# Convolution of a fused recurrent kernel: products over 64 rows on both halves of PE in place of products over 128 rows with a zero block

## The chip, the cores and the metric

One NeuronCore of one Trainium2 chip. The metric is the device time of one execution in microseconds, median of three runs. The kernel is bound by TensorE (PE), which holds a stationary operand of up to 128 x 128 and streams a moving operand through it. VectorE (DVE), ScalarE (ACT) and GpSimd (POOL) do the elementwise work, SyncE (SP) issues all DMAs.

## The reference, cut to what matters

Two layers over x of shape (128 batch, 128 time, 512 channels), float32. The change touches the first one, and in it the convolution, its projection, and the order of a few steps at the end of the projection.

```python
# layer 0: K = 128 taps, conv_w = cond (128 taps, 512 channels), N = 64
x_pad = jnp.pad(x, ((0, 0), (K - 1, 0), (0, 0)))
conv = conv_b + sum((x_pad[:, k:k + L, :] * conv_w[k, 0] for k in range(K)))
proj = conv @ Wp + bp
B_t = jax.nn.softplus(proj[..., :N])
C_t = jnp.tanh(proj[..., N:])
u = x @ Ws + bs
state = decay * state + dt * b_t * u_t        # scan over 128 steps, y = c_t * state
x = x + y @ Wo + bo
# layer 1
h_next = jnp.tanh(h @ Wh + x_t @ Wx + b)      # scan over 128 steps
x = x + h
```

The convolution is causal and depthwise, and has as many taps as there are time steps: for each channel it is a product of a lower triangular Toeplitz matrix (128 x 128) with x of that channel (128 times x 128 batch).

## The kernel before, in words

The program has two stages. The first (up to about 298 us) computes the convolution and its projection for all times into `bc` (128 rows x 16384, in SBUF), in four chunks of 128 channels. The second (from about 298 us to the end) walks the 32 groups of four time steps through both recurrences. The change touches the first stage only.

**Convolution** (`convolution`, lines 717 to 737). For each channel there is one float32 matmul: the stationary operand is `x_ring` (128 times in reverse order x 128 batch), the moving one `t_ring` (128 x 128, a band of the Toeplitz matrix). A float32 matmul runs as two pairs of a weight load and a matmul instruction, so 512 channels give 1024 of each (line 734). Four channels fill one PSUM bank. The banks are taken in turn from `CONV`, four of the eight, and bank m may be rewritten when bank m - 4 has been copied out. Even banks are copied to `conv` by ACT (`copy_conv`, line 380), odd ones by DVE (line 545), each with 512 elements on 128 rows.

The band of a channel is made of two halves of 128 rows x 64 columns. A DMA brings the half with late times. Of the half with early times, the lower 64 rows are copies of the upper 64 rows of the other half, made by DVE (`fill_band`, line 536, one copy of 64 x 512 for 8 channels), and the upper 64 rows are a zero block, set once for each of the eight ring slots by DVE (line 514). So a quarter of what is streamed is zeros.

**The ring.** `t_ring` and `x_ring` have eight slots of 8 channels. SP issues two DMAs for a slot (`load_ring`, 256 KB from `hankel` with an overlapping access pattern, `band`, and 512 KB from `x_rev`) as soon as the matmuls of the slot's last use are done.

**Turning and projecting** (`split_projection`, lines 739 to 763). When a chunk is through, PE transposes `conv` (line 747, four transposes for one step m of 32), ACT rounds the result to `turned_hi`, DVE makes the rest `turned_lo`, and three matmuls of 512 columns follow, three steps behind (lines 757 to 759). Even results are added into `bc` by DVE (`add_even`), odd ones are copied by ACT to `projected`, which lies in the space of `conv`, and added by POOL (line 316). Because of that shared space ACT and DVE wait for all of POOL's adds (`odd_added`) before they write `conv` again. PE waits for the copies of n = 28 and 29 at the end, as the next convolution writes banks 0 to 3. The last chunk is projected with plain float32 matmuls (`last_projection`, from line 827: transposes on line 844, two instructions of 512 columns for a step on line 851), with DVE adding each step into `bc` (line 552).

**Set in by hand in the last projection:** the softplus of the first 8 time groups (`soft_abs` on DVE, `soft_exp` and `soft_ln` on ACT, `soft_sum` on DVE), the first group's u, v, state and y, and `y_copy(0)` on ACT after step 31, on which DVE's `y_rest(0)` waits. Every engine runs its instructions in the order of the program, and orders between engines are semaphores.

## Time and profile before

| what | value |
|---|---|
| median of 3 runs | 1181.77 us (1181.17 to 1183.36) |
| profiled execution, its own time | 1181.11 us |
| its span in the profile | 1179.3 us |
| PE busy / weight loads busy | 1149.5 us (97%) / 954.1 us (81%) |
| DVE, ACT, POOL busy | 712.8, 558.5, 369.0 us |
| chain that ended last, share of PE | 95% |

A busy time is the time in which at least one instruction of the engine is running. Matmul instructions overlap, since a new one starts while the last drains; the pace of a stage is therefore its busy time over its instructions, not the mean duration of one.

### The profile page before, as it was taken

What the parts mean: (1) busy time and instruction counts of PE and PEld (TensorE: products, weight loads), DVE (VectorE), ACT (ScalarE), POOL (GpSimd) and SP (SyncE); (2) the same over time, 40 slices, a digit from 0 to 9 for tenths busy, and PEclk for the clock granted to TensorE, in tenths of its full rate; (3) what the DMA queues carried; (4) which work ended last, traced back from release to release, by engine and by line L of the source; (5) the groups of instructions that cost most, each with busy time, mean ns of one, the idle gap of its engine ahead of it and who ended that gap; (6) DMA issues with size and microseconds to landing.
All of it is one profiled execution on the core that took longest, in us unless ns stands there. A gap on an engine that the chain in (4) does not pass through costs nothing.

```text
span 1179.3 us, 16686 instructions
## 1 busy us (share of the span) xinstructions
PE 1149.5 (97%) x5984; PEld 954.1 (81%) x5984; DVE 712.8 (60%) x1154; ACT 558.5 (47%) x819; POOL 369.0 (31%) x214
## 2 busy tenths in 40 slices
PE   5999999998999999999999999999999999999997
PEld 5889898975788888888888888888888888888886
DVE  5786868667655555556556565555555655556553
ACT  2574837545345445453545454544545354545431
POOL 1000514225133333333333333333333333333330
PEclk9999999999999999999999999999999999999999
DMA  9919084551122222222222222222322222222202
GB/s 317 334 43 359 33 290 141 179 169 36 37 72 72 72 77 96 86 94 73 71 71 71 71 71 71 71 71 78 96 85 94 74 71 71 71 71 72 72 36 72
DMA packets 81471, 121.29 MB, mean 103 GB/s; under 512 B 3936, under 2 KB 39776, under 8 KB 81440
## 3 DMA queue, kind: packets, MB, share of 16 engines
q1 hardware_dynamic: 81440, 120.87, 31.7%
q8 instruction: 20, 0.33, 0.1%
q14 instruction: 11, 0.09, 0.0%
HBM read 87.30 MB, written 33.55 MB: 102 GB/s over the span
## 4 chain that ended last, share of the span: by engine, by line
PE 95%; DVE 2%; DMA 1%; issue 0%; ACT 0%; POOL 0%; SPq 0%; POOLq 0%; DVEq 0%; ACTq 0%
PE bank L812 10%; PE bank L734 10%; PE bank L820 10%; PE bank L821 10%; PE bank L806 10%; PE bank L824 10%; PE bank L805 10%; PE bank L874 5%; PE bank L747 3%; PE bank L779 3%; PE bank L785 3%; PE bank L795 2%; PE bank L796 2%; PE bank L757 2%; PE bank L758 2%; PE bank L759 2%
## 5 line engine op out<-in xcount | busy, mean ns | idle before, releaser
L352 POOL TENSOR_TENSOR x_lo<-x_f,x_hi 128x512 fp32r<-128x512 f32 x124 | 156.6, 1295 | 556.7 <-ACT x_hi L454 556.7
L488 ACT ACTIVATE h_f<-z_f 128x512 f32<-128x512 f32 x128 | 80.9, 632 | 295.1 <-DVE z_f L683 295.1
L693 DVE TENSOR_TENSOR hT_lo<-bank,hT_hi 128x512 fp32r<-128x512 f32 x128 | 88.6, 692 | 187.7 <-ACT hT_hi L492 187.7
L820 PE MATMUL bank<-wh_hi,hT_hi 128*128 128x512 f32 x512 | 200.4, 391 | 0.0
L821 PE MATMUL bank<-wh_lo,hT_hi 128*128 128x512 f32 x512 | 199.9, 390 | 0.0
L806 PE MATMUL bank<-wx_lo,x_hi 128*128 128x512 f32 x512 | 199.6, 390 | 0.0
L805 PE MATMUL bank<-wx_hi,x_hi 128*128 128x512 f32 x512 | 199.2, 389 | 0.0
L683 DVE TENSOR_TENSOR z_f<-bank,b_rows 128x512 f32<-128x512 f32 x128 | 88.6, 692 | 130.2 <-PE bank L824 129.4
L346 POOL TENSOR_TENSOR x_lo<-x_f,x_hi 128x2048 fp32r<-128x2048 f32 x32 | 147.7, 4615 | 13.9 <-ACT x_hi L459 13.9
L812 PE MATMUL bank<-wx_hi,x_lo 128*128 128x512 f32 x512 | 144.8, 404 | 0.3 <-POOL x_lo L352 0.3
L824 PE MATMUL bank<-wh_hi,hT_lo 128*128 128x512 f32 x512 | 137.1, 389 | 0.0
L734 PE MATMUL bank<-t_ring,x_ring 128*128 128x128 f32 x1024 | 119.8, 277 | 13.1 <-DVE t_ring L536 12.3
L734 PEld LDWEIGHTS bank<-t_ring,x_ring 128*128 128x128 f32 x1024 | 118.5, 190 | 14.8 <-issue 14.1
L492 ACT CAST hT_hi<-bank 128x512 fp32r<-128x512 f32 x128 | 75.1, 587 | 95.5 <-PE bank L874 95.5
L820 PEld LDWEIGHTS bank<-wh_hi,hT_hi 128*128 128x128 f32 x512 | 96.1, 188 | 26.0 <-ACT hT_hi L492 6.1
L454 ACT CAST x_hi<-x_f 128x512 fp32r<-128x512 f32 x128 | 79.6, 622 | 77.6 <-DVE x_f L645 75.3
L824 PEld LDWEIGHTS bank<-wh_hi,hT_lo 128*128 128x128 f32 x512 | 96.1, 188 | 20.4
L805 PEld LDWEIGHTS bank<-wx_hi,x_hi 128*128 128x128 f32 x512 | 96.1, 188 | 19.9
L806 PEld LDWEIGHTS bank<-wx_lo,x_hi 128*128 128x128 f32 x512 | 96.1, 188 | 19.9
L821 PEld LDWEIGHTS bank<-wh_lo,hT_hi 128*128 128x128 f32 x512 | 96.2, 188 | 19.5
L812 PEld LDWEIGHTS bank<-wx_hi,x_lo 128*128 128x128 f32 x512 | 91.2, 188 | 17.3 <-POOL x_lo L352 0.6
L645 DVE SCALAR_TENSOR_TENSOR x_f<-bank,vec,x_f 128x512 f32<-128x512 f32 x128 | 89.9, 744 | 4.9 <-PE bank L796 4.5
(89 smaller groups left out, 1632.1 us busy)
## 6 DMA issues: line engine op xcount, KB each, us to landing
x_ring<-x_rev SPq DMA_DIRECT2D x64, 512.0 KB, 8.4
x_f<-x_dtb SPq DMA_DIRECT2D x32, 1024.0 KB, 8.3
out<-x_f SPq DMA_DIRECT2D x31, 1024.0 KB, 5.4
t_ring<-hankel SPq DMA_DIRECT2D x64, 256.0 KB, 7.6
w_f<-Wx SPq DMA_DIRECT2D x1, 1024.0 KB, 5.5
w_f<-Wh SPq DMA_DIRECT2D x1, 1024.0 KB, 5.2
out<-x_f SPq DMA_DIRECT2D x4, 256.0 KB, 2.3
turned<-Wp SPq DMA_DIRECT2D x3, 128.5 KB, 2.1
```

What stands on the lines that cost most here:

```text
L346: nc.gpsimd.tensor_tensor(x_lo[:], x_f[:, par], f(x_hi[:]), ALU.subtract).then_inc(xlo_ready, 1)
L352: nc.gpsimd.tensor_tensor(x1_lo[:, c], x1_f[:, par, c], f(x1_hi[:, c]), ALU.subtract)\
L645: nc.vector.scalar_tensor_tensor(out=x1_f[:, par, c].rearrange("p t b -> p (t b)"), in0=XB[c][:], scalar=bo_c[:, c:c + 1], in1=x_f[:, par, ...
L683: nc.vector.tensor_tensor(z_f[:], ZB[s % 2][:], b_rows[:], ALU.add).then_inc(zsum_ready, 1)
L693: nc.vector.tensor_tensor(hT_lo[:], turned_h, f(hT_hi[:]), ALU.subtract).then_inc(htlo_ready, 1)
L734: mm = nc.tensor.matmul(CONV[m % 4][:, bass.ts(d % PER_BANK, TIME)], x_ring[:, slot, d % CH], t_ring[:, slot, d % CH // 2, :, d % 2], star ...
L805: nc.tensor.matmul(z, x1_hi[:, k, s], wx_hi[:, k], start=start and k == 0, stop=False)
L806: nc.tensor.matmul(z, x1_hi[:, k, s], wx_lo[:, k], start=False, stop=False)
L812: mm = nc.tensor.matmul(z, x1_lo[:, k, s], wx_hi[:, k], start=False, stop=stop and k == KC - 1)
L820: nc.tensor.matmul(z, hT_hi[:, k], wh_hi[:, k], start=start and k == 0, stop=False)
L821: nc.tensor.matmul(z, hT_hi[:, k], wh_lo[:, k], start=False, stop=False)
L824: mm = nc.tensor.matmul(z, hT_lo[:, k], wh_hi[:, k], start=False, stop=stop and k == KC - 1)
```

## The change

1. A channel's product is cut by rows. For channel k of a pair (k = 0 or 1) a product over 64 rows gives all 128 times (`early`, 128 columns), and a second one over the other 64 rows only the late 64 times (`late`, 64 columns); the zero block isn't computed or stored. Channel 0 of a pair has its early product on rows 64 to 127 and its late one on rows 0 to 63, channel 1 the other way round (the host swaps the row halves of every second channel). The order for two channels is early 0, early 1, late 0, late 1.
2. The two products go to different banks. Four channels take a pair of banks, and the four pairs are all eight banks: products of rows 64 to 127 go to the first bank of a pair, products of rows 0 to 63 to the second. ACT copies the 512 early elements of every m, then DVE adds the 256 late ones onto them in `conv`. PE waits for DVE alone.
3. The bands are laid out in full by the host (`bands`, one contiguous row of 512 elements for each partition and 8 channels) and DVE's fill becomes two copies of 64 x 256. The zeroing is gone.
4. The next convolution starts on the banks used for turning, and waits for the last four projected banks at m = 2 and m = 3. In chunks 1 and 2, DVE adds the last two odd steps too, and POOL adds 14 and not 16. All loops over chunks are written out.
5. In the last projection the softplus steps are split and set earlier, `y_copy(0)` goes before the last turned copy, and one more add of DVE before `y_rest(0)`.

```diff
-        CONV, TURN, PROJ = bank[0:4], bank[4:6] + bank[0:2], bank[2:4] + bank[6:8]
+        bank_pair = [ctx.enter_context(nc.psum_tensor(f"bank_pair{i}", [P, 2, 512], F32)) for i in range(4)]
+        bank = [bank_pair[i // 2][:, i % 2] for i in range(8)]
+        CONV = [bank_pair[i] for i in (2, 0, 1, 3)]
+        TURN, PROJ = bank[4:6] + bank[0:2], bank[2:4] + bank[6:8]
...
-            t_ring = sb(first, "t_ring", [P, RING, CH // 2, TIME, 2])
+            t_ring = sb(first, "t_ring", [P, RING, 2, 2, 2, 2, N])
...
-                sp.dma_start(t_ring[:, slot, :, N:, :].rearrange("p j l i -> p j (l i)"), band(n))\
+                sp.dma_start(t_ring[:, slot, 1].rearrange("p a i k l -> p (a i k l)"), bands[bass.ds(n * P, P), :])\
...
-                for n in range(1, BANKS, 2):
-                    pool.wait_ge(odd_copied, BANKS // 2 * c + n // 2 + 1)
+                for n in range(1, BANKS - 4, 2):
+                    pool.wait_ge(odd_copied, ODD * (c - 1) + BANKS // 2 + n // 2 + 1)
...
             def copy_conv(c):
-                with act.Fori(0, BANKS // 4) as i:
-                    m = 4 * i
-                    for k in (0, 2):
-
-                        act.wait_ge(conv_done, BANKS * c + m + k + 1)
-                        nc.scalar.copy(conv[:, :, bass.ds((m + k) * PER_BANK, PER_BANK)],
-                                       CONV[k][:].rearrange("p (d l) -> p l d", d=PER_BANK)).then_inc(conv_copied_act, 1)
+                for m in range(BANKS):
+                    act.wait_ge(conv_done[0], BANKS * c + m + 1)
+                    act.wait_ge(conv_done[1], BANKS * c + m + 1)
+                    nc.scalar.copy(conv[:, :, bass.ts(m, PER_BANK)].rearrange("p l (i k) -> p k i l", k=2),
+                                   CONV[m % 4][:, :, 0:2 * TIME].rearrange("p k (i l) -> p k i l", i=2))\
+                      .then_inc(conv_copied_act, 1)
...
-                if m == 8:
-                    soft_exp(0, soft[0])
-                    soft_exp(1, soft[1])
-                if m == 10:
-                    soft_ln(0, soft[0])
-                    soft_ln(1, soft[1])
+                if m in (7, 8):
+                    soft_exp(m - 7, soft[m - 7])
+                    soft_ln(m - 7, soft[m - 7])
...
-            y_copy(0)
+                if m == 30:
+                    y_copy(0)
...
-            for slot in range(RING):
-                nc.vector.memset(t_ring[0:N, slot, :, 0:N, :], 0.0).then_inc(t_zero, 1)
...
-                nc.vector.tensor_copy(t_ring[N:P, slot, :, 0:N, :].rearrange("p j l i -> p j (l i)"),
-                                      t_ring[0:N, slot, :, N:, :].rearrange("p j l i -> p j (l i)")).then_inc(t_full, 1)
+                for k, (early, late) in enumerate(((slice(N, P), slice(0, N)), (slice(0, N), slice(N, P)))):
+                    nc.vector.tensor_copy(t_ring[early, slot, 0, :, :, k], t_ring[late, slot, 1, :, :, k]).then_inc(t_full, 1)
...
-                for n in range(P // CH):
-                    if n + 1 < P // CH:
-                        fill_band(c, n + 1)
-                    m = 2 * n + 1
-                    dve.wait_ge(conv_done, BANKS * c + m + 1)
-                    nc.vector.tensor_copy(conv[:, :, bass.ts(m, PER_BANK)],
-                                          CONV[m % 4][:].rearrange("p (d l) -> p l d", d=PER_BANK))\
-                      .then_inc(conv_copied_dve, 1)
+                for m in range(BANKS):
+                    if m % 2 == 0 and m // 2 + 1 < P // CH:
+                        fill_band(c, m // 2 + 1)
+                    dve.wait_ge(conv_copied_act, BANKS * c + m + 1)
+                    sums = conv[:, N:, bass.ts(m, PER_BANK)].rearrange("p l (i k) -> p k i l", k=2)
+                    late = CONV[m % 4][:, ::-1, 2 * TIME:3 * TIME].rearrange("p k (i l) -> p k i l", i=2)
+                    nc.vector.tensor_tensor(sums, late, sums, ALU.add).then_inc(conv_copied_dve, 1)
...
-            dve.wait_ge(odd_added, BANKS // 2)
+            dve.wait_ge(odd_added, ODD)
...
-                if m == 4:
-                    dve.wait_ge(proj_added, 4)
-                    for n in range(2 * EARLY):
-                        soft_abs(n, n % 2, soft[n // 2])
-                if m in (9, 10):
+                if m in (2, 4):
+                    q = m // 2 - 1
+                    dve.wait_ge(proj_added, m)
+                    for n in (2 * q, 2 * q + 1):
+                        soft_abs(n, n % 2, soft[q])
+                if m in (6, 7):
                     for par in range(2):
-                        soft_sum(m - 9, 2 * (m - 9) + par, par, soft[m - 9])
+                        soft_sum(m - 6, 2 * (m - 6) + par, par, soft[m - 6])
...
             last_add(25)
+            last_add(26)
             y_rest(0)
-            for m in (26, 27, 30, 31):
+            for m in (27, 30, 31):
...
+                def early(slot, pair, k, i, to):
+                    rows = slice(0, N) if k else slice(N, P)
+                    return nc.tensor.matmul(to[:, k, bass.ts(i, TIME)].rearrange("p (h l) -> p h l", h=2),
+                                            x_ring[rows, slot, 4 * pair + 2 * i + k], t_ring[rows, slot, :, pair, i, k],
+                                            start=True, stop=True)
+
+                def late(slot, pair, k, i, to):
+                    rows = slice(N, P) if k else slice(0, N)
+                    return nc.tensor.matmul(to[:, 1 - k, 2 * TIME + i * N:2 * TIME + (i + 1) * N],
+                                            x_ring[rows, slot, 4 * pair + 2 * i + k], t_ring[rows, slot, 1, pair, i, k],
+                                            start=True, stop=True)
...
+                    if m in (2, 3) and released:
+                        for freed in (BANKS - 4, BANKS - 3) if m == 2 else (BANKS - 2, BANKS - 1):
+                            released(freed)
+                    if m >= 4:
+                        pe.wait_ge(conv_copied_dve, BANKS * c + m - 3)
+                    for i in range(2):
+                        early(slot, pair, 0, i, to)
+                        early(slot, pair, 1, i, to)
+                        last_of_top = late(slot, pair, 0, i, to)
+                        last_of_bottom = late(slot, pair, 1, i, to)
+                    last_of_top.then_inc(conv_done[0], 1)
+                    last_of_bottom.then_inc(conv_done[1], 1)
```

## Rows read from the trace of the kernel before

**Rows 1.** The page: busy time of PE, and the chain that ended last
```profile
PE 1149.5 (97%) x5984; PEld 954.1 (81%) x5984; DVE 712.8 (60%) x1154; ACT 558.5 (47%) x819; POOL 369.0 (31%) x214
...
PE 95%; DVE 2%; DMA 1%; issue 0%; ACT 0%; POOL 0%; SPq 0%; POOLq 0%; DVEq 0%; ACTq 0%
```

**Rows 2.** Groups of instructions by line and form, 0 to 340 us (busy, mean ns | idle before)
```profile
L734 PE MATMUL bank<-t_ring,x_ring 128*128 128x128 f32 x1024 | 119.8, 277 | 13.1 <-DVE t_ring L536 12.3 <-issue 0.7
L734 PEld LDWEIGHTS bank<-t_ring,x_ring 128*128 128x128 f32 x1024 | 118.5, 190 | 14.8 <-issue 14.1 <-DVE t_ring L536 0.5
...
L545 DVE COPY conv<-bank 128x512 f32<-128x512 f32 x64 | 44.3, 692 | 46.4 <-PE bank L734 46.4
...
L380 ACT COPY conv<-bank 128x512 f32 x64 | 37.5, 586 | 80.5 <-PE bank L734 80.5
...
L536 DVE COPY t_ring<-t_ring 64x512 f32<-64x512 f32 x64 | 28.2, 440 | 7.0 <-POOL bc L316 4.0 <-POOL wo_lo L301 1.2
```

**Rows 3.** Stretches of convolution, line 734 alone (length, PE, weight loads, clock, DMA, GB/s)
```profile
15.80:42.90 27.10, 27.08 (x238) 26.92 (x238) 1.00 1.07 360
85.20:110.60 25.40, 25.40 (x225) 25.40 (x224) 1.00 1.06 353
```

**Rows 4.** Timeline: first convolution product and first transpose after a pause (start, duration)
```profile
81.34 0.19 PEld L734 LDWEIGHTS bank<-t_ring,x_ring 128*128 128x128 f32 x1 [0.39 <-issue]
81.35 0.38 PE L734 MATMUL bank<-t_ring,x_ring 128*128 128x128 f32 x1
...
44.13 0.14 PEld L747 LDWEIGHTS bank<-ident,conv 128*128 128x128 f32 x1 [1.00 <-ACT conv L380]
44.16 0.30 PE L747 MATMUL bank<-ident,conv 128*128 128x128 f32 x1 [0.83 <-issue]
```

**Rows 5.** The chain in order of time, 0 to 260 us (start, length)
```profile
43.33 0.83 issue
...
81.40 29.46 PE bank L734 x256
...
217.17 1.81 PE bank L734 x16
...
219.70 27.46 PE bank L734 x240
...
251.37 0.86 PE bank L851 x2
```

**Rows 6.** Timeline around the start of the third chunk's convolution
```profile
148.34 2.67 POOL L316 TENSOR_TENSOR bc<-bc,conv 128x512 f32<-128x512 f32 x2 [0.53 <-ACT conv L399]
...
149.11 2.08 PE L734 MATMUL bank<-t_ring,x_ring 128*128 128x128 f32 x16
...
151.04 0.42 DVE L536 COPY t_ring<-t_ring 64x512 f32<-64x512 f32 x1 [1.98 <-POOL bc L316]
...
151.51 4.69 PE L734 MATMUL bank<-t_ring,x_ring 128*128 128x128 f32 x39 [0.32 <-DVE t_ring L536]
```

**Rows 7.** Timeline, 287 to 290 us: short instructions of DVE
```profile
287.62 0.74 DVE L608 SCALAR_TENSOR_TENSOR u_sum<-bank,vec,u_lo 64x512 f32<-64x512 f32 x1 [1.77 <-ACT u_lo L425]
...
289.12 0.22 DVE L619 COPY s_f<-v_f 64x128 f32<-64x128 f32 x1
...
289.38 1.13 DVE L623 SCALAR_TENSOR_TENSOR s_f<-s_f,rates,v_f 64x128 f32<-64x128 f32 x3
```

**Rows 8.** Timeline of the last projection: PE's pauses and what DVE does
```profile
262.26 1.13 PE L851 MATMUL bank<-turned,wp_now 128*128 128x512 f32 x2 [0.51 <-ACT turned L405]
...
267.68 5.10 DVE L602 SCALAR_TENSOR_TENSOR bc<-bc,x_f 64x512 f32<-64x512 f32 x2
...
273.65 1.10 PE L851 MATMUL bank<-turned,wp_now 128*128 128x512 f32 x2 [3.34 <-DVE bc L552]
...
295.69 1.95 PE L851 MATMUL bank<-turned,wp_now 128*128 128x512 f32 x4 [1.23 <-DVE bc L552]
```

**Rows 9.** All instructions of line 602 (shortest/median/longest ns)
```profile
L602 DVE SCALAR_TENSOR_TENSOR bc<-bc,x_f x4: 673/1536/4299, 264.0 to 272.0; 64x512 f32<-64x512 f32 x4
```

More of the change, by code:

```diff
@@ L34, in wait, with build @@
         engine.wait_ge(sem, value)
-def build(nc, x_rev, x_dtb, hankel, h0_t, vectors, Wp, Ws, Wo, Wx, Wh, b, out):
+def build(nc, x_rev, x_dtb, bands, h0_t, vectors, Wp, Ws, Wo, Wx, Wh, b, out):
     ctx = ExitStack()
@@ L385, in turned_to_hi @@
                 for m in range(BANKS + LAG + 1):
-                    if m > LAG and m % 2:
+                    if m > LAG and m % 2 and (c == 0 or m - LAG - 1 < BANKS - 4):
                         copy_odd(c, m - LAG - 1)
@@ L715, in _ @@
             pe.wait_ge(ident_ready, 1)
-            def convolution(c):
-                for d in range(P):
-                    slot, m = (d // CH) % RING, d // PER_BANK
-                    if d % CH == 0:
-                        pe.wait_ge(t_zero, slot + 1)
-                        pe.wait_ge(t_full, P // CH * c + d // CH + 1)
-                        pe.wait_ge(xr_loaded[slot], DMA * (P // CH // RING) * c + DMA * (d // CH // RING + 1))
-                    if d % PER_BANK == 0 and m >= 4:
-                        if m % 2 == 0:
-                            pe.wait_ge(conv_copied_act, BANKS // 2 * c + (m - 4) // 2 + 1)
-                        else:
-                            pe.wait_ge(conv_copied_dve, BANKS // 2 * c + (m - 4) // 2 + 1)
-                    mm = nc.tensor.matmul(CONV[m % 4][:, bass.ts(d % PER_BANK, TIME)], x_ring[:, slot, d % CH],
-                                          t_ring[:, slot, d % CH // 2, :, d % 2], start=True, stop=True)
-                    if d % PER_BANK == PER_BANK - 1:
-                        mm.then_inc(conv_done, 1)
@@ L739, in split_projection, with convolution @@
-            def split_projection(c):
-                half = BANKS // 2
-                pe.wait_ge(conv_copied_act, half * (c + 1))
-                pe.wait_ge(conv_copied_dve, half * (c + 1))
+            def convolution(c, released=None):
+                def early(slot, pair, k, i, to):
[8 more added lines that the diff above has]
+                                            start=True, stop=True)
+                for m in range(BANKS):
+                    n, pair = m // 2, m % 2
+                    slot, to = n % RING, CONV[m % 4]
+                    if pair == 0:
+                        pe.wait_ge(t_full, 2 * (P // CH * c + n + 1))
+                        pe.wait_ge(xr_loaded[slot], DMA * (P // CH // RING) * c + DMA * (n // RING + 1))
+                    if m in (2, 3) and released:
[10 more added lines that the diff above has]
+                    last_of_bottom.then_inc(conv_done[1], 1)
@@ L752, in split_projection @@
                         if n >= 4:
-                            pe.wait_ge(odd_copied if n % 2 else even_added, half * c + (n - 4) // 2 + 1)
-                        if n == 3:
-                            wait(pe, odd_copied, half * c)
+                            released(n - 4)
                         hi, lo = wp_hi[:, bass.ts(n % 2, P)], wp_lo[:, bass.ts(n % 2, P)]
@@ L760, in split_projection @@
                           .then_inc(proj_done, 1)
-                pe.wait_ge(even_added, half * (c + 1) - 1)
-                pe.wait_ge(odd_copied, half * (c + 1) - 1)
-            convolution(0)
-            split_projection(0)
-            with pe.Fori(1, KC - 1) as c:
-                convolution(c)
-                split_projection(c)
-            convolution(KC - 1)
-            pe.wait_ge(odd_copied, BANKS // 2 * (KC - 1))
-            pe.wait_ge(even_added, BANKS // 2 * (KC - 1))
+                return released
+            released = None
+            for c in range(KC - 1):
+                convolution(c, released)
+                released = split_projection(c)
+            convolution(KC - 1, released)
             def u_first(g):
@@ L905, in halves @@
         return np.concatenate([a, a], axis=0)
+    lags = np.concatenate([zeros, cond[::-1].T, zeros[:, :1]], axis=1)
+    windows = lags[:, N + np.arange(P)[:, None] + np.arange(N)[None]]
+    x_rev = x.transpose(1, 2, 0)[::-1].copy()
+    swapped = np.arange(1, D, 2)
+    windows[swapped] = windows[swapped][:, other]
+    x_rev[:, swapped] = x_rev[other][:, swapped]
     arrays = {
-        "x_rev": x.transpose(1, 2, 0)[::-1],
+        "x_rev": x_rev,
         "x_dtb": x.transpose(2, 1, 0),
-        "hankel": np.concatenate([zeros, cond[::-1].T, zeros[:, :1]], axis=1).reshape(D // 2, 2, 2 * P).swapaxes(1, 2),
+        "bands": windows.reshape(D // CH, CH, P, N).transpose(0, 2, 1, 3).reshape(D // CH * P, CH * N),
         "h0_t": cond.T,
```

46 lines of the change are left out of this document (29 added, 17 removed).

## The prediction

> **What bounds the kernel now.** I read the page first. PE is busy for 97% of the span and holds 95% of the chain [rows 1], so what counts is PE's time and PE's pauses. Then the groups by line in the first 340 us. The convolution keeps PE busy for 119.8 us, a tenth of the kernel, with 1024 weight loads beside 1024 matmul instructions, while DVE and ACT, which copy its results, need 0.69 and 0.59 us for a bank and wait for PE most of the time [rows 2]. The stretches without a pause give the pace: 25.40 us for 224 or 225 pairs is 0.1134 us for a pair of load and product, both rows at 100% and the clock at 1.00, that is 2.4 GHz [rows 3]. A channel is two pairs, 0.227 us.
>
> The question that decides is which of the two sets this pace. Two rows tell it. A pair of projection instructions with 512 columns each takes 0.86 us [rows 5], so an instruction streams 512 columns in 0.43 us, 128 in 0.107 and 64 in 0.054 us. The loads: after a pause the first product of a convolution stands at 81.35 for 0.38 us, 0.10 us longer than the usual 0.275; it was waiting for weights whose load had begun at 81.34. A transpose in the same place is only 0.03 us longer than its usual 0.27 [rows 4]. So a convolution's load lasts about 0.11 us by itself, as long as the 128 columns take. Loads and products run side by side, at 0.1134 us each, and making the products shorter leaves the loads.
>
> **The change, part by part.**
>
> PE in the convolution. For two channels there were 4 pairs of load and product: 4 x 0.1134 = 0.454 us. Now there are 8, four on each half of the rows: two with 128 columns, two with 64. No row shows a product over 64 rows, nor two halves at work together, so this is bounded from both sides. Below: the halves run fully beside each other and a load over 64 rows is short enough to hide. Then a half needs 2 x 0.113 + 2 x 0.060 = 0.347 us. Above: nothing overlaps, 8 x 0.1134 = 0.907 us. Between them: the halves overlap, and each load keeps its 0.1134 us, since it still carries 128 batch columns; a half has 4 loads, so 0.454 us, exactly as now. I take this value, because it is what the nearest row [rows 3] gives for the number of loads on one half. **Streaming a quarter less is worth nothing** if the loads set the pace: 0 us over 256 pairs of channels. The Trainium skill (TensorE: Matmul & The Clock Gate, section LDWEIGHTS) says that a load's time goes by its columns and not its rows, at 107 ns for 128; the 0.10 us above agrees, and no run here shows it for 64 rows.
>
> The copies. For every 4 channels PE takes 0.907 us. ACT now copies all of them (0.586 us each by line 380), and stays under. DVE adds 256 elements: a three-operand instruction goes from 0.38 us (1.13 for three, 128 elements) to 0.74 us (512 elements) [rows 7], 0.94 to 1.02 ns an element, so the 692 ns of line 545 become about 0.43 us. The fill in two copies of 256 lies between 0.22 (128 elements, rows 7) and 0.44 us (512, rows 2) each, say 0.29, so 0.58 instead of 0.44 for 8 channels. DVE's work is 0.43 + 0.29 = 0.72 us for 4 channels, 23 us in a chunk against PE's 29. Both engines are covered by PE; without that cover DVE's 0.72 us is the next bound. A set of banks comes back after some 1.4 us of copy and add, and PE needs it after 2.7: no wait.
>
> At the end of each convolution the transposes need everything copied. PE's pause there is 0.83 us [rows 5], of which DVE's copy is 0.69. Now ACT (0.59) and DVE (0.43) follow each other: 0.33 more and a second handover of about 0.1. Four chunks: **+1.7 us**. If the add took all of 0.69 it would be +2.8.
>
> At the start of a chunk's convolution PE pauses before its second group of 8 channels. POOL's last two adds end at 151.01, only then does DVE fill the second band, and PE starts at 151.51, 0.59 us after 149.11 + 1.81 [rows 6]. In the fourth chunk it is 219.70 - 217.17 - 1.81 = 0.72 us [rows 5], and in the second the whole stretch lasts 29.46 us [rows 5] where 256 x 0.1134 is 29.03, 0.4 us more. With two adds fewer POOL is through before DVE wants to go on; DVE has two adds more (2 x 0.69), and can fill at about 149.9, ready by 150.5, before the 150.9 at which PE comes. **-1.7 us**. The missing loop code and the wait for two banks that is no longer there give a few tenths more, 3 x 0.15: **-0.5 us**.
>
> The zeroing, 8 instructions at the start, lies before the wait for the first DMA and is worth nothing; the second fill copy lengthens the start by 0.2 us, counted as nothing. The bands bring the same bytes, 256 KB, in longer rows; the DMAs already run at 353 to 360 GB/s [rows 3], and this rate has room: 768 KB are 2.2 us, a slot is refilled once in eight groups. SP's waits for two semaphores instead of one are on the same matmuls.
>
> The last projection. PE has three pauses: 0.51, 3.34 and 1.23 us [rows 8], 5.1 in all. The second comes from `soft_sum` on DVE, where two instructions took 5.10 us beside POOL's splitting of Wh, while the shortest of the four took 0.67 [rows 8, 9]. Earlier, at m = 6 and 7, they fall into the time in which POOL waits for Wh, and cost 0.7 to 1.5 each. Set in pairs with adds between them they leave DVE at most about 4 us behind, which the four banks nearly cover: 0.7 us of new pause (0 to 3). The third pause is DVE waiting for `y_copy(0)`; with that copy one step earlier it goes, and what is late next is add 27, just in time. **-4.4 us** (-5 to -1.5). The 880 us of the recurrence are untouched.
>
> Sum: 0 + 1.7 - 1.7 - 0.5 - 4.4 = -4.9 us on the profiled execution's 1181.1 (span 1179.3 and 1.8 around it), which stands 0.7 under the median. That gives 1176 us. The small terms alone leave 1173 to 1181.
>
> **The rivals.**
>
> *The halves take turns* (slower). A float32 product is two instructions with two loads, so the order of the change on the two halves, B and T, is B B T T T T B B. If an instruction can't start before the one ahead of it has started, T's first can run beside B's second, but B's next must wait for T's last. Of 8 slots 6 remain in sequence: 6 x 0.1134 = 0.680 us for two channels, +0.227, and over 256 pairs +58 us: 1176 + 58 = 1234. For it: loads and products keep the order of the program wherever the timeline shows them, and the four instructions on T are back to back, a load each. Against it: nothing, as no row has two halves. It decides as soon as starts are in order. The Trainium skill (TensorE: Matmul & The Clock Gate, section Packing small matmuls) says that products start and end in the order of the program even on different rows, which by its rule is this case, while the page TensorEngine Tiling (Array Packing), section Key Properties, says that tiles work independently, loads included, which is my forecast.
>
> *In turns, but with short loads.* If a load over 64 rows hides behind 64 columns, the six slots are 3 of 0.113 and 3 of 0.060: 0.52 us, +0.065, over 256 pairs +17 us: 1193.
>
> *The change doesn't do what it says.* If the halves don't overlap, or their loads share one path, it is 0.907 us for two channels, +116 us: 1292. Against it speaks only that this would leave half the array idle at any time.
>
> *The loads are shorter on half the rows* and the halves independent. Then PE needs 22 us for a chunk, DVE 23 becomes the bound, 6 us gained in each of three chunks. In the first one the ring is limited by its DMAs, 12.6 MB at 360 GB/s are 35 us from the start, and about 4 us are gained. -22 us: 1154. For it: rows 3 can't tell a pace set by loads from one set by products by more than a few ns. Against it: the 0.10 us of rows 4.
>
> **How the numbers follow.** Independent halves with the pace of the loads 0.30, shorter loads 0.22, in turns 0.26, in turns with short loads 0.10, no overlap 0.12. The forecast is the first, 1176. A measurement here can tell 0.2%, 2.4 us. The first case lies 4.9 + 0.7 us under the median with an error of some 4, so it gives 0.25 of its 0.30 to faster, 0.04 to the same, 0.01 to slower; the second is faster, the other three slower: faster 0.47, same 0.04, slower 0.49. The range goes from the shorter loads (1154 and a little) to the halves in turns (1234 and the upper end of the small terms), 1152 to 1239, and leaves out the case without overlap. Cases of both signs hold most of the chance; the likeliest one alone has 1173 to 1181.
>
> **What would show it.** In the stretches of convolution the pace: 4 channels in 0.91 us is the forecast, 1.36 in turns, 1.04 in turns with short loads, 1.81 without overlap, 0.72 with shorter loads and DVE at its limit. PE's row then holds 2048 loads, and products of both halves should start within a few ns of each other, if independent; in turns, only one in four does. PE's pause before the first transpose should be about 1.25 us; the pauses before a chunk's second group should be gone; in the last projection PE should stand for under 1.5 us in all, and line 602 should show 0.7 to 1.5 us. I am wrong if the pace of the convolution isn't 0.454 us for two channels, or if DVE's add takes much more than 0.43 us and PE waits for it.

## The result and the profile after

The kernel with the change takes **1217.9 us** (median of 4 runs, 1217.4 to 1218.66), and the kernel before, beside it on the same chip, 1182.57. The ratio is 1.0298, with a 95% interval of 1.0286 to 1.0310: slower by 35 us, where 1176 was predicted. The profiled execution has a span of 1215.6 us at a mean granted clock of 0.997, 36.3 us more than before.

The page: busy times, then the chain.

```profile
PE 1162.6 (96%) x7008; PEld 959.1 (79%) x7008; DVE 768.2 (63%) x1278; ACT 642.2 (53%) x879; POOL 363.8 (30%) x210
...
PE 87%; ACT 6%; DVE 5%; issue 1%; DMA 1%; POOL 0%; SPq 0%; POOLq 0%; ACTq 0%; DVEq 0%
```

PE held 95% of the chain before [rows 1] and holds 87% now; ACT and DVE have 11% of it, some 134 us, where they had 2% before. The groups by line and form, 0 to 340 us, show where:

```profile
L380 ACT COPY conv<-bank_pair 128x512 f32<-128x512 f32 x128 | 123.4, 1035 | 34.4 <-PE bank_pair L726 32.5
L720 PE MATMUL bank_pair<-t_ring,x_ring 64*128 64x128 f32 x1024 | 119.1, 310 | 31.4 <-DVE t_ring L535 31.3
L544 DVE TENSOR_TENSOR conv<-bank_pair,conv 128x256 f32<-128x256 f32 x128 | 88.7, 714 | 26.0 <-ACT conv L380 25.2
L726 PE MATMUL bank_pair<-t_ring,x_ring 64*128 64x64 f32 x1024 | 87.9, 248 | 0.0
...
L535 DVE COPY t_ring<-t_ring 64x256 f32<-64x256 f32 x128 | 38.8, 303 | 4.0
```

ACT's copy of 512 elements takes 1035 ns, where the same shape took 586 [rows 2]. DVE's add takes 714 ns, where 430 ns were predicted. And PE's idle time before `early` (line 720) is 31.4 us, ended by DVE's fill of the band.

PE itself does what was forecast. The timeline of PE in a stretch without a pause (start, length):

```profile
101.58 0.34 PE L726 MATMUL bank_pair<-t_ring,x_ring 64*128 64x64 f32 x4
...
102.19 0.44 PE L720 MATMUL bank_pair<-t_ring,x_ring 64*128 64x128 f32 x4
102.47 0.34 PE L726 MATMUL bank_pair<-t_ring,x_ring 64*128 64x64 f32 x4
102.64 0.44 PE L720 MATMUL bank_pair<-t_ring,x_ring 64*128 64x128 f32 x4
```

Two channels are four instructions of line 720 and four of line 726. The next two channels begin 0.45 us later (102.19 and 102.64), which is 4 times the 0.1134 us of [rows 3]. The starts of the single instructions in the trace show that a product of the top half and one of the bottom half start 7 ns apart.

The chain between 96.6 and 101.8 us, in order of time (start, length), shows what PE waits for:

```profile
96.64 0.49 PE bank_pair L720 x4
97.13 0.17 PE bank_pair L726 x4
97.30 0.28 PE bank_pair L720 x4
97.58 0.23 PE bank_pair L726 x3
...
97.88 0.85 ACT conv L380
...
98.78 1.05 ACT conv L380
...
99.84 0.71 DVE conv L544
...
100.59 0.29 DVE t_ring L535
...
100.91 0.30 DVE t_ring L535
...
101.25 0.49 PE bank_pair L720 x4
```

This is a **ring of dependences**, a loop of waits that leads back to the engine where it began. It closes once in 16 channels: PE computes four channels (1.17 us), ACT copies them (0.85 us of it behind PE's last product) and the next four (1.05), DVE adds to these (0.71), and only then fills in two copies (0.29 + 0.30) the band with which PE may go on. With 0.24 us between the steps it closes at 101.25, 4.61 us after 96.64. In that time PE does 16 channels, 3.63 us at the pace of before (16 x 0.227). The fill doesn't depend on the add: it stands behind it on DVE's queue.

The sum, up to the first transposes of the last projection, which start at 281.18 against 248.13: 33.05 us later. By the starts of PE's instructions in the two traces it has three parts. The four stretches of convolution, from first to last product, are 147.5 us long in all against 119.7, +27.8. In each of them PE pauses seven times, and a ring closes at each pause: 28 x (4.61 - 3.63) = 27.4 us. The pauses before a chunk's second group, which are gone, give 1.7 us back, as predicted. Of the 2 us that this leaves open, most are in the first chunk. The pauses before the transposes are 1.98 us each, where they were 0.83, 0.97, 0.97 and 0.99: +4.2. And the first product starts at 13.28 and not at 11.99: +1.3. That is 33.3, within 0.3 of the whole.

The late start is that of the first band, which now needs two copies. The chain from 9 to 14 us:

```profile
11.10 0.73 DVE t_ring L535
...
11.86 1.33 DVE t_ring L535
...
13.28 0.76 PE bank_pair L720 x3
```

The second copy lasts 1.32 us, where one with nothing beside it takes 0.29: it began 0.09 us after an add of POOL's that lasted 1.26. Before, the band needed one copy, and it took 0.86 us. So the start costs 2.08 - 0.86 = 1.2 us more. All nine traces with 64-row products show the 1.32 us there.

From there to the first product with `u` (284.56 before, 322.28 now) it is 41.1 us instead of 36.4, +4.7, and the rest is 1.4 us shorter: 33.05 + 4.7 - 1.4 = 36.3.

The +4.7 stand in the timeline of the last projection:

```profile
281.18 1.94 PE L858 MATMUL bank_pair<-ident,conv 128*128 128x128 f32 x16 [1.98 <-ACT conv L380]
...
286.97 4.53 POOL L324 TENSOR_TENSOR wx_lo<-w_f,wx_hi 128x2048 fp32r<-128x2048 f32 x1
...
287.22 5.01 DVE L592 TENSOR_SCALAR x_f<-bc 64x512 uint32<-64x512 uint32 x2
...
297.60 6.58 DVE L599 SCALAR_TENSOR_TENSOR bc<-bc,x_f 64x512 f32<-64x512 f32 x2
...
298.79 4.84 POOL L328 TENSOR_TENSOR wh_lo<-w_f,wh_hi 128x2048 fp32r<-128x2048 f32 x1
...
305.05 2.04 PE L865 MATMUL bank_pair<-turned,wp_now 128*128 128x512 f32 x2 [4.61 <-DVE bc L549]
```

One `soft_abs` began beside POOL's splitting of Wx and one `soft_sum` beside that of Wh, and each lasted as long as POOL did. PE stood for 4.61 us, and after that pause two products take 2.04 us instead of 1.10 [rows 8]. The windows of PE's granted clock say why the products are slow (length, PE, clock, DMA share, GB/s):

```profile
305.00:309.00 4.00, 3.96 (x8) 0.50 0.63 163
309.00:313.00 4.00, 4.00 (x18) 0.88 0.27 103
```

The clock was at 1.2 GHz for the first four microseconds and for part of the next four. That costs 4 x 0.50 + 4 x 0.12 = 2.5 us. PE's pauses in this projection are 0.90, 0.36 and 4.61 us in place of 0.51 and 3.34, which is another 2.0 us; the two are the +4.7 but for 0.2.

### The profile page after: what moved, and what is told of

It reads as the page before. It is cut to its first block, busy times and chain, and to the rows that moved or that the text cites. A ratio compares the mean times of both kernels' runs of the same rounds, so it can differ in the third digit from the quotient of the medians.

```text
span 1215.6 us, 18767 instructions
## 1 busy us (share of the span) xinstructions
PE 1162.6 (96%) x7008; PEld 959.1 (79%) x7008; DVE 768.2 (63%) x1278; ACT 642.2 (53%) x879; POOL 363.8 (30%) x210
## 4 chain that ended last, share of the span: by engine, by line
PE 87%; ACT 6%; DVE 5%; issue 1%; DMA 1%; POOL 0%; SPq 0%; POOLq 0%; ACTq 0%; DVEq 0%
PE bank_pair L826 10%; PE bank_pair L834 10%; PE bank_pair L835 10%; PE bank_pair L820 10%; PE bank_pair L838 9%; PE bank_pair L819 9%; ACT conv L380 5%; PE bank_pair L888 5%; PE bank_pair L767 3%; PE bank_pair L799 2%; PE bank_pair L793 2%; PE bank_pair L809 2%; PE bank_pair L810 2%; PE bank_pair L720 2%; PE bank_pair L775 2%; PE bank_pair L776 2%
## 5 line engine op out<-in xcount | busy, mean ns | idle before, releaser
L834 PE MATMUL bank_pair<-wh_hi,hT_hi 128*128 128x512 f32 x512 | 200.4, 391 | 0.0
L835 PE MATMUL bank_pair<-wh_lo,hT_hi 128*128 128x512 f32 x512 | 199.8, 390 | 0.0
L820 PE MATMUL bank_pair<-wx_lo,x_hi 128*128 128x512 f32 x512 | 199.6, 390 | 0.0
L819 PE MATMUL bank_pair<-wx_hi,x_hi 128*128 128x512 f32 x512 | 199.2, 389 | 0.0
L720 PE MATMUL bank_pair<-t_ring,x_ring 64*128 64x128 f32 x1024 | 119.1, 310 | 31.4 <-DVE t_ring L535 31.3
L826 PE MATMUL bank_pair<-wx_hi,x_lo 128*128 128x512 f32 x512 | 144.8, 404 | 0.3 <-POOL x_lo L354 0.3
L380 ACT COPY conv<-bank_pair 128x512 f32<-128x512 f32 x128 | 123.4, 1035 | 34.4 <-PE bank_pair L726 32.5
L838 PE MATMUL bank_pair<-wh_hi,hT_lo 128*128 128x512 f32 x512 | 137.1, 389 | 0.0
L834 PEld LDWEIGHTS bank_pair<-wh_hi,hT_hi 128*128 128x128 f32 x512 | 96.1, 188 | 26.0 <-ACT hT_hi L492 6.1
L835 PEld LDWEIGHTS bank_pair<-wh_lo,hT_hi 128*128 128x128 f32 x512 | 96.2, 188 | 19.4
```

Source lines behind the costliest of these rows:

```text
L380: nc.scalar.copy(conv[:, :, bass.ts(m, PER_BANK)].rearrange("p l (i k) -> p k i l", k=2), CONV[m % 4][:, :, 0:2 * TIME].rearrange("p k (i ...
L720: return nc.tensor.matmul(to[:, k, bass.ts(i, TIME)].rearrange("p (h l) -> p h l", h=2), x_ring[rows, slot, 4 * pair + 2 * i + k], t_ring[ ...
L819: nc.tensor.matmul(z, x1_hi[:, k, s], wx_hi[:, k], start=start and k == 0, stop=False)
L820: nc.tensor.matmul(z, x1_hi[:, k, s], wx_lo[:, k], start=False, stop=False)
L826: mm = nc.tensor.matmul(z, x1_lo[:, k, s], wx_hi[:, k], start=False, stop=stop and k == KC - 1)
L834: nc.tensor.matmul(z, hT_hi[:, k], wh_hi[:, k], start=start and k == 0, stop=False)
```

## The experiments

Two theories. **The ring**: the time is set by ACT's copy, DVE's add and the fills in series, long because the copy and the add walk `conv` in a new order (line 380 had four channels innermost, 16 bytes in a row; it now has a channel's times innermost, each 512 bytes from the last; in the PSUM banks, from which it reads, it is the new order that takes neighbouring elements). **The rival**: PE is slowed by its products over half the rows, and the copies are only seen to wait for it.

**The order of ACT's copy alone.** The same elements, channels innermost:

```diff
-  conv[:, :, bass.ts(m, PER_BANK)].rearrange("p l (i k) -> p k i l", k=2)
-  CONV[m % 4][:, :, 0:2 * TIME].rearrange("p k (i l) -> p k i l", i=2)
+  conv[:, :, bass.ts(m, PER_BANK)].rearrange("p l (i k) -> p l i k", k=2)
+  CONV[m % 4][:, :, 0:2 * TIME].rearrange("p k (i l) -> p l i k", i=2)
```

> ACT's copy of the convolution walks times outside and the four channels inside, as the kernel before did, so that it writes 16 bytes in a row instead of 4 bytes every 512. Nothing else changes. My theory: the copy's 1.03 us in the changed kernel comes from this order, so line 380 falls to about 0.59 us, and the ring of dependences (PE's four channels, two copies on ACT, DVE's add, two fills, PE four steps later), 4.62 us in the changed kernel, loses 2 x 0.4 us: about 3.8 us for four steps, 26 us off 1218, near 1191. Rival: the copy is slow because it reads two PSUM banks in one instruction; then line 380 stays at 1.03 us and the time at 1218.

**The order of DVE's add alone**, by the same edit in `sums` and `late`:

> The same change of order in DVE's add alone; ACT's copy stays as in the changed kernel. My theory: the add falls from 0.71 us to about 0.43, and since it stands in the ring once, four steps go from 4.62 to about 4.33 us: 9 us off, near 1209. Rival: ACT's throughput (four copies in 3.92 us) is the bound and not the ring; then a shorter add changes nothing, 1218. Third: the add isn't slow by its order, stays at 0.71, 1218.

**Both orders:**

> Both orders changed. My theory: the ring is 0.89 + 0.3 + 1.18 + 0.43 + 0.61 + handovers, about 3.5 us, just under PE's own 4 x 0.894 = 3.58 us for four steps, so PE comes to set the pace of the convolution: 32 x (4.62 - 3.6) = 33 us off, near 1185. Rival (PE's halves are what slowed it): 1210 or more. The copies still add up to a longer pause before the transposes than in the kernel before, so it won't be under 1180.

Measured: 1201.34 us, ratio 1.0168 [1.0151, 1.0185]; 1206.55, 1.0213 [1.0196, 1.0230]; 1191.68, 1.0091 [1.0074, 1.0108]. One row of the groups from each of the first two, ACT's with its order and DVE's with its own:

```profile
L380 ACT COPY conv<-bank_pair 128x512 f32<-128x512 f32 x128 | 74.9, 585 | 67.9 <-PE bank_pair L726 67.9
```

```profile
L544 DVE TENSOR_TENSOR conv<-bank_pair,conv 128x256 f32<-128x256 f32 x128 | 54.3, 425 | 50.9 <-ACT conv L380 50.0
```

The order in which elements are walked, and nothing else, makes 1035 ns into 585 and 714 into 425, which are the 586 and 430 of the prediction. Since the quick order takes elements from far apart in PSUM, from two banks in turn, and the slow one takes neighbours there, the price lies on the side of `conv` in SBUF. The ring shrinks with the two instructions. In the chains it takes 4.16 us with ACT's order (92.19 to 96.35), 4.32 with DVE's (93.93 to 98.25), 3.87 with both. From 4.61, 28 rings save 12.6, 8.1 and 20.7 us, and the pauses before the transposes, now 1.55, 1.71 and 1.28 us and not 1.98, save 1.7, 1.1 and 2.8. That makes 14.3, 9.2 and 23.5; by the ratios the kernels save 15.4, 10.0 and 24.5. DVE's order alone was expected to give 9 us and did; ACT's was expected to give 26 and both together 33, which is more than they gave. The chain of the kernel with both orders shows why:

```profile
92.13 0.49 PE bank_pair L720 x4
...
94.26 0.59 ACT conv L380
...
94.88 0.43 DVE conv L544
...
95.34 0.29 DVE t_ring L535
...
95.65 0.30 DVE t_ring L535
...
96.00 0.49 PE bank_pair L720 x4
```

Now ACT waits for PE's second step of four channels, which ends 2.1 us after the ring's start, so the ring runs through PE, one copy, one add and the fills, and is still 0.24 us longer than 16 channels. With quick copies there are still 11 us left, and most of them lie in the fill's place on DVE, as the runs with earlier fills will show.

**The fills earlier, the slow orders kept:**

```diff
-  if m % 2 == 0 and m // 2 + 1 < P // CH:
-      fill_band(c, m // 2 + 1)
+  if m % 2 == 0 and m // 2 + 2 < P // CH:
+      fill_band(c, m // 2 + 2)
```

(The first two bands of a chunk are filled before it.)

> DVE fills the bands two groups ahead instead of one; both copies keep the slow order. My theory of the ring: with the fill out of it what is left is throughput, ACT 4 x 0.98 = 3.92 us and DVE 4 x 0.71 + 4 x 0.30 = 4.05 us for four steps, so about 4.1 us instead of 4.62: 16 us off, near 1201. Rival: the bound is the slow copy alone, wherever the fill stands; then nothing changes, 1218.

Measured: 1198.22 us, 1.0141 [1.0124, 1.0158], near the expected 1201. The ring is open, and ACT is the bound. The chain of 90 to 130 us by line, and ACT's copies in a window of it (length, ACT, clock, DMA share, GB/s):

```profile
by line: ACT conv L380 70.6%; PE bank_pair L769 13.3%; issue 5.0%; PE bank_pair L778 4.0%; PE bank_pair L777 4.0%; PE bank_pair L779 3.6%; ACTq L379 0.4%
```

```profile
95.00:120.00 25.00, 23.59 (x25) 1.00 1.02 385
```

Two copies take 2.00 us from start to start, and the eight channels that they copy take PE 1.79. DVE is nearly as full as ACT (19.07 and 19.46 of the 20 us from 95 to 115), but ACT is the one that never waits there. Against the next kernel, which has the quick orders too, the four stretches of convolution are 11.2 us longer by the traces (127.7 and 116.5) and the pauses before the transposes 2.8 (4 x 0.7). That is 14.0 of the 16.5 us by which this kernel comes later to its last projection (263.22 and 246.68). Its first product is 0.5 us later, and after the pauses of 1.98 us in the second and third chunk its clock fell to 0.50 for 3.4 us each time, which the next kernel's did not.

**Both orders and the fills earlier:**

> Both orders changed and the bands filled two groups ahead; the last projection as in the changed kernel. In e3 the ring is 3.87 us for four steps (PE two steps and their drain 2.1, ACT 0.59, DVE 0.43, fills 0.61, handovers). With the fill out of it PE's own pace, 4 x 0.894 = 3.58 us, should be left: 32 x 0.29 = 9 us off e3's 1191.7, near 1183. If PE's halves can't hold 0.447 us for two channels through a whole stretch, it stays at 1188 or more.

Measured: 1183.40 us, 1.0002 [0.9994, 1.0011]. All of the 35 us are gone with 64-row products, in the order of the change, still in the kernel. The rival falls. In the traces the four stretches of convolution take 147.5 us in the changed kernel, 125.3 with quick orders alone, 127.7 with early fills alone and 116.5 with both. So the slow orders alone cost 11 us, the fill's place alone 9, and the two together 31: more than their sum, because the slow instructions stand in the ring.

```profile
L722 PE MATMUL bank_pair<-t_ring,x_ring 64*128 64x128 f32 x1024 | 115.9, 303 | 12.6 <-DVE t_ring L535 12.6
```

PE's idle time before a convolution's products is 12.6 us, the 13.1 of before [rows 2] which is mostly the kernel's start. But the kernel is only level with before, not 5 us faster, so something else gives back what was expected to be gained.

**The same with the old last projection** (the softplus, `y_copy` and the last adds as before):

> As e5, and the last projection's steps back in the order of the kernel before. From the first transpose of the last projection to the first group's u the changed kernel took 41.1 us, the kernel before 36.4. My theory: the new order lays one abs and one sum of DVE beside POOL's two long splits, each of which stops DVE for the length of a POOL instruction, where the old order laid only sums there. So this run is 3 to 5 us faster than e5, near 1179. Rival: the new order is harmless and the difference comes from later loads of Wx and Wh after the slower convolution; then e6 equals e5 within 1 us.

Measured: 1180.84 us, 0.9983 [0.9974, 0.9993]. From the first transposes to `u` it is 36.3 us instead of 42.1. The total falls by less, 2.6 us where 3 to 5 were expected: in the two profiled executions 1.2 us go back at the start, where the first product comes at 13.75 and not 12.56, and 1.3 behind `u`, where the late `y_copy` is.

**The new last projection alone, in the kernel before:**

> The kernel before with part 5 of the change alone (softplus steps split and earlier, y_copy earlier, one add earlier). My prediction had 4.4 us gained here. What e5 against e6 says: the new places of the softplus steps cost 2.6 us, and e6 against e10 that the early y_copy and add gain 2.3. Together about 0: 1181 to 1184. If the loss in the changed kernel came only from its later loads, this run should be 2 to 4 us under the kernel before instead.

Measured: 1184.12 us, 1.0008 [0.9997, 1.0018]: no gain, where the prediction had -4.4 us. The chain of 245 to 300 us has the two instructions that POOL holds up:

```profile
255.21 4.63 DVE x_f L593
...
267.30 4.88 DVE bc L600
```

**Half the columns, all the rows**: the kernel before with products of 64 columns. It leaves out the early half of the convolution, whose part of PSUM is zeroed once, so it is no kernel to use. It measures by itself whether loads or columns set the pace.

```diff
-  nc.tensor.matmul(CONV[m % 4][:, bass.ts(d % PER_BANK, TIME)], x_ring[:, slot, d % CH],
-                   t_ring[:, slot, d % CH // 2, :, d % 2], ...)
+  nc.tensor.matmul(CONV[m % 4][:, d % PER_BANK * TIME + N:(d % PER_BANK + 1) * TIME], x_ring[:, slot, d % CH],
+                   t_ring[:, slot, d % CH // 2, N:, d % 2], ...)
```

> The kernel before with only 64 of the 128 columns streamed in each convolution product (the late times; the early half of the convolution is left out, its PSUM columns are zeroed once). The weight loads are the same 1024 of 128 x 128. Theory: the loads set the pace, so line 734 keeps 0.113 us an instruction and the time stays within 2 us of the kernel before, 1180 to 1183. Rival: the products set it; then an instruction takes 0.06 us and the convolution loses up to 12 us a chunk, until its DMAs (2.2 us for 8 channels) or copies bound it: 1150 or less.

Measured: 1207.03 us, 1.0203 [1.0188, 1.0218], where 1180 to 1183 was expected. In the second and third chunk the starts of the instructions lie 0.1117 us apart, against 0.1134 with 128 columns: half the streaming is worth 1.5% of the pace, so the loads set it, as the prediction took it. But the chunks differ (line of the products, windows of PE in the second and the fourth chunk):

```profile
107.00:130.00 23.00, 23.00 (x208) 1.00 0.96 319
...
250.00:290.00 40.00, 40.00 (x189) 0.50 0.38 125
```

In the fourth the granted clock stood at 0.50, 1.2 GHz, and an instruction took 0.2133 us though PE never paused. The first chunk ran at the same pace, 54.8 us for its 256 instructions. What its clock was, this trace doesn't tell: a window reads 1.00 where there is no record, and the first record of the clock begins at 70.63 us, behind that chunk. (In the kernel before it begins at 15.88 us, and that is where the pace goes from some 0.21 us an instruction to 0.1133.) A window of the first chunk (length, PE, weight loads, DVE, clock, DMA share, GB/s):

```profile
45.00:50.00 5.00, 5.00 (x25) 5.00 (x25) 0.42 (x1) 1.00 0.83 257
```

The profiled execution is longer than the others of this kernel. It took 1229.87 us at a mean clock of 0.973, and the other four 1206.04 to 1207.27 at 0.995 to 0.998. The first chunk is 23.4 us longer than before and the fourth 23.0. So an estimate from these numbers is that the four executions, some 24 us above the kernel before, had one slow chunk, the first; they left no trace that could show it. Fewer columns with the same loads gained nothing, and in the trace the lower clock stood through a whole chunk of them.

**The order on the two halves**: both early products, then both late ones on the bottom first, so that starts in the order of the program would put two instructions of a half behind each other.

```diff
-  early(slot, pair, 0, i, to)
-  early(slot, pair, 1, i, to)
-  last_of_top = late(slot, pair, 0, i, to)
-  last_of_bottom = late(slot, pair, 1, i, to)
+  early(slot, pair, 0, i, to)
+  last_of_bottom = late(slot, pair, 1, i, to)
+  early(slot, pair, 1, i, to)
+  last_of_top = late(slot, pair, 0, i, to)
```

> As e5 (orders and fills mended), but the four products of two channels are issued as bottom, bottom, top, top rows instead of bottom, top, top, bottom. Theory: each half of the rows works through its own products whatever stands between them, so the pace stays 0.447 us for two channels and the time that of e5, 1183. Rival (starts in the order of the program): the top half then begins only when the bottom half's last product has begun; in the weakest form the two halves share one start in four and two channels take up to 0.8 us, 1220 to 1270.

Measured: 1183.24 us, 1.0007 [0.9998, 1.0017], level with the other order (1183.40). The timeline of PE:

```profile
94.85 0.49 PE L722 MATMUL bank_pair<-t_ring,x_ring 64*128 64x128 f32 x4
95.12 0.39 PE L728 MATMUL bank_pair<-t_ring,x_ring 64*128 64x64 f32 x4
95.29 0.49 PE L722 MATMUL bank_pair<-t_ring,x_ring 64*128 64x128 f32 x4
```

0.44 us for two channels, though the starts of the two halves now lie 55 ns apart instead of 7. The halves don't take turns in any order tried.

**What the small parts are worth.** First `y_copy(0)` one step earlier and add 26 ahead of `y_rest(0)`, alone in the kernel before:

> The kernel before with y_copy(0) and the add of step 26 earlier, and nothing else. Theory: PE's last pause in the projection (1.2 us) goes, 1 to 2 us faster than the kernel before, near 1181.

Then this on the mended kernel with the old softplus placement:

> As e6, but of the new last projection two steps are kept: y_copy(0) ahead of the last turned copy, and the add of step 26 ahead of y_rest(0). Theory: PE's last pause of 1.2 us goes: 1 to 1.2 us faster than e6, near 1178. This is the candidate for the best of both. Rival: the copies of steps 30 and 31 then come late for PE, and it equals e6.

And last the kernel before with its own 128-row convolution, and of the change only this, the two adds moved from POOL to DVE and PE's loop over the chunks written out:

> The kernel before with e11's edit and the other small part: POOL adds 14 odd steps in chunks 1 and 2, DVE the last two, and the loop over chunks written out. Convolution with 128 rows as before. Theory: the pauses before the second group (1.7 us in all) go as well, so 3 us under the kernel before, near 1179.5, and level with e10 (1178.5): then the 64-row products have brought nothing, as loads set the pace either way. Rival: e10's gain is the halves', and this one stays 2 us or more above it.

Measured: 1181.14 us, 0.9988 [0.9979, 0.9997]; **1178.50**, 0.9972 [0.9961, 0.9983]; **1179.29**, 0.9969 [0.9957, 0.9981]. The last two both beat the kernel before and the changed one, by 0.3% of the former. In the mended kernel's chain PE's pause of 1.23 us [rows 8] is gone:

```profile
291.93 3.45 PE bank_pair L869 x8
```

and in the last kernel's timeline so is the pause before the third chunk's second group, which stood between 149.11 and 151.51 [rows 6]:

```profile
148.65 4.62 PE L737 MATMUL bank<-t_ring,x_ring 128*128 128x128 f32 x37
```

The two kernels differ in the convolution's form. The 64-row form reaches the last projection at 247.65, the 128-row form at 246.43, 1.2 us earlier. By the traces this is a balance. The four stretches of convolution are 1.8 us shorter with 64 rows (116.5 and 118.4), since two channels take 0.447 us there and 0.453 here. Its pauses before the transposes are 1.6 us longer in all (1.28 each, against 0.83 three times and 0.99), and its first product starts 1.6 us later (13.53 and 11.90), 1.2 of it by the second fill copy beside POOL. The medians don't show the 1.2 us. In the profiled execution of the 128-row kernel PE's clock dropped after the pause at `soft_sum` and in the other it did not, which takes 3.0 us; whether that is so in the other executions no trace tells:

```profile
271.80:276.00 4.20, 4.15 (x8) 0.50 0.75 225
```

```profile
272.80:276.00 3.20, 3.14 (x14) 1.00 0.58 156
```

(windows of PE just after that pause, 3.29 us long in both). So what was gained is the work of the small parts: the 64-row products brought 1.8 us in their pace, and their copies and their start took it back.

## Why the prediction was wrong, and where it was right

**The failed step** is "The copies": "ACT now copies all of them (0.586 us each by line 380), and stays under", DVE's "692 ns of line 545 become about 0.43 us", and from these "Both engines are covered by PE" and "a set of banks comes back after some 1.4 us of copy and add, and PE needs it after 2.7: no wait". It failed twice.

First, the price. The rows from which it was taken have the same elements in another order. They measured 1035 and 714 ns, and 585 and 425 with the order put back. With 1.00 us for a copy against PE's 0.89 for four channels ACT alone is above PE (the experiment with early fills: 11 us more of convolution, and 3 in the pauses), and the cover is gone.

Second, the loop. The prediction checked one loop, the banks, and not the other that runs through the same engines: the next band is filled behind add m-1 on DVE's queue, and that add waits for ACT's copy. With the predicted prices this ring would have been 3.87 us, as the kernel with both orders shows, still 0.24 over PE's 3.63; it needed both the price and the place to become 28 x 0.98 = 27.4 us. What is queued behind a waiting instruction was asked of SP and not of DVE. The prediction's last sentence named the symptom ("DVE's add takes much more than 0.43 us and PE waits for it"), at no chance of its own.

The Trainium skill bears on the price: SBUF — State Buffer, section "Door 1: The DMA port swizzle", says in a note that consecutive accesses within one 16-byte line, four float32 values, go at full bandwidth and that each crossing to a new line costs extra. The measured 585 against 1035 and 425 against 714 ns agree with its direction; it gives no amount.

**The pace of PE: right.** 0.45 us for two channels, predicted 0.454. The halves are independent and the loads set the pace (0.1134 us with 128 columns, 0.1117 with 64). No limit on the issue of instructions sets it, as with two halves at work a pair of load and product begins every 0.056 us. "The halves take turns", at 1234 us, was the rival nearest to the measured time, with a mechanism that isn't there; its variant at 1193, "the loads are shorter on half the rows" and the case without overlap fall by the same pace. The Trainium skill (TensorE: Matmul & The Clock Gate, section "The mechanism") has products start and end in program order even on different rows. The equal times of two orders, 1183.40 and 1183.24 us, show that such an order, if it holds here, costs nothing. The page TensorEngine Tiling (Array Packing) of the Trainium skill, section "Key Properties", has tiles independent, and the runs agree.

**The pause before the transposes: right in the mended kernel, too small in this one.** Predicted 1.25 us; measured 1.28 where the copies have their old price, and 1.98 with 1.04 for the copy and 0.71 for the add. The increase was predicted on 0.83 in all four chunks, which only the first had; the others had 0.97 to 0.99. With the old prices the pauses are therefore 1.4 us longer in all and not 1.7.

**The pauses before a second group: right**, and so was the reason, fewer adds on POOL: the stretches of the second to fourth chunk are 1.6 us shorter in the kernel with the small parts alone than in the kernel before. **The start was put at 0.2 us and counted as nothing**; it took 1.3, of which the second fill copy, caught beside POOL, is 1.2.

**The last projection: -4.4 predicted, +3.3 measured** (+4.7 and -1.4). Of its parts `y_copy` was right: PE's 1.23 us went. The softplus step was wrong: "they fall into the time in which POOL waits for Wh, and cost 0.7 to 1.5 each". Line 599's four instructions took 1978 ns in the mean, one of them 4.89 us, and the `soft_abs` moved ahead to m = 2 and 4 met POOL's other splitting, of Wx, which the prediction never looked at, for 4.47 us on the chain. Before, the first of the four took 2.84 us beside that splitting, where the others took 0.42, and PE didn't wait; now it pauses for 0.90 us. The Trainium skill (SBUF — State Buffer, section "SBUF: two separate sides") says that DVE and POOL share a pair of ports under an exclusive lock, which the first to start holds for its whole instruction; it names two kinds of DVE instruction that need it, those in a two-port mode and those with two inputs in SBUF. `soft_sum` has two such inputs, and its row agrees: an instruction with the work of 0.67 us [rows 9] lasts 4.89 beside one of POOL's of 4.84 that had begun 0.50 us before it. To it comes the dip in PE's clock, 2.5 us, that no step had.

**The range** held the result only because it reached to cases that did not happen. The prediction gave 0.49 to slower, but 0.48 of it to mechanisms of PE that none of the runs show: that the sign was among the likely ones is luck.

## What to carry to other kernels

Take the duration of a copy from a row with the same shape, type **and order of elements**; where the change turns the access pattern, the row is no measure of the new copy, and here it was 1.7 times too low. When an engine's work gets longer, write down every loop of waits that passes through it, with the instructions that only stand behind it in its queue, and compare each loop's sum with the bound engine's time for the same work. And before making products smaller, find out whether the columns or the weight loads set the pace.

## What the runs showed of the hardware

- Order of elements, same data: ACT's copy of 128x512 from PSUM to SBUF takes 585 ns when it writes 16 bytes in a row and 1035 when it writes 4 bytes every 512, though the slow order reads neighbours in PSUM. DVE's add over 128x256 takes 425 and 714 ns.
- A load of 64 rows by 128 columns costs as much as one of 128 rows: 0.112 us (a stretch of 256 starts on each half in 28.53 us), against 0.1117 to 0.1134. Loads of the two halves go on beside each other.
- Beside an instruction of POOL that both reads and writes SBUF, two instructions of DVE lasted until it ended: 4.89 us in place of 0.67, and 4.55 in place of 0.42. A fill copy began beside a shorter one and took 1.32 us in place of 0.29.
- With half the columns to stream and unchanged loads PE never paused in the fourth chunk, and still the granted clock was 0.50 from 244.71 to 299.32 us. The first chunk had the same pace of 0.2133 us, without a record of the clock.
- After a pause of 3.29 us the clock was at 0.50 for another 6.0 us in one kernel (270.98 to 277.81) and stayed at 1.00 in another. What decides this stays open.
